# A decoder layer on one core: attention's x turned by a transfer instead of TensorE, and the keys scaled earlier

## What is computed

```python
x = x + mamba(layernorm(x))              # in-projection, causal conv, one 64-token chunk, gated norm, out-projection
x = x + xattn(layernorm(x), ctx_2048)    # 16 query heads, 4 key/value heads of 128
x = x + ffn(layernorm(x))                # 256 -> 1024 -> 256, activations rounded to 8 bits, ternary weights

def xattn(h, e):
    q = (h @ Wq + bq).reshape(..., 16, 128)
    k = (e @ Wk + bk).reshape(..., 4, 128)
    v = (e @ Wv + bv).reshape(..., 4, 128)
    q, k = rmsnorm(q) * qn_w, rmsnorm(k) * kn_w
    p = softmax(q @ k.T / sqrt(128) + mask)
    return (p @ v) @ Wo
```

## Time and profile before

| | us |
|---|---|
| median of 3 runs | 1190.26 (1189.74 to 1191.51) |
| the profiled execution | 1191.23 |
| its span | 1189.5 |
| TensorE busy | 1119.2 (94%) |
| VectorE busy | 1005.5 (85%) |
| GpSimd busy | 935.8 (79%) |
| ScalarE busy | 819.7 (69%) |

### The profile page before, as it was taken

How to read it: one execution, slowest core, us unless ns; L and a number is a source line. 1 busy time by engine, 2 the same in 40 slices (tenths; PEclk the granted TensorE clock), 3 DMA queues, 4 the chain that set the end, 5 groups by cost and what they waited for, 6 DMA issues and landing times.

```text
span 1189.5 us, 34826 instructions
## 1 busy us (share of the span) xinstructions
PE 1119.2 (94%) x11405; PEld 983.7 (83%) x11405; DVE 1005.5 (85%) x2509; ACT 819.7 (69%) x2066; POOL 935.8 (79%) x1514
## 2 busy tenths in 40 slices
PE   4889999999999999999999999999999999999964
PEld 3678888898888889888888988888898888888753
DVE  4766898898889889888988988898898889888666
ACT  4586777677667767766776776677677667766641
POOL 4788788888888888888888888888888888878651
PEclk8899999999999999999999999999999999999987
DMA  8311101111110111111011111101111110121000
GB/s 297 87 50 24 33 17 31 37 37 35 33 37 15 29 37 37 35 33 37 15 29 37 37 35 33 37 15 29 37 37 35 33 37 15 29 35 30 22 9 23
DMA packets 103306, 46.31 MB, mean 39 GB/s; under 512 B 80352, under 2 KB 101600, under 8 KB 103008
## 3 DMA queue, kind: packets, MB, share of 16 engines
q1 hardware_dynamic: 100336, 45.75, 14.8%
q10 hardware_dynamic: 2928, 0.03, 0.1%
HBM read 23.93 MB, written 4.19 MB: 24 GB/s over the span
## 4 chain that ended last, share of the span: by engine, by line
PE 66%; DVE 13%; ACT 13%; issue 4%; POOL 2%; DMA 1%; ACTq 1%; POOLq 0%; DVEq 0%; SPq 0%
PE bank L1800 18%; PE bank L1882 5%; PE bank L1860 5%; PE bank L1718 4%; PE bank L1690 4%; PE bank L1691 4%; PE bank L1692 4%; DVE hh L1389 3%; DVE hh L1382 3%; ACT kb L875 3%; PE bank L1813 3%; PE bank L1940 2%; PE bank L1707 2%; PE bank L1870 2%; PE bank L1762 2%
## 5 line engine op out<-in xcount | busy, mean ns | idle before, releaser
L1800 PE MATMUL bank<-xcT,wq 128*128 128x128 f32 x2048 | 234.1, 275 | 2.2 <-ACT xcT L862 2.2
L1800 PEld LDWEIGHTS bank<-xcT,wq 128*128 128x128 f32 x2048 | 231.2, 192 | 2.9 <-issue 2.5
L1223 DVE SCALAR_TENSOR_TENSOR xc<-bank,cw,xc 128x124 f32<-128x124 f32 (+2 forms) x576 | 163.7, 339 | 11.6 <-ACT xc L831 3.0
L1690 PE MATMUL bank<-wo_hi,o_hi 128*128 128x256 f32 x512 | 149.5, 292 | 1.1 <-DVE o_lo L1312 1.1
L1691 PE MATMUL bank<-wo_lo,o_hi 128*128 128x256 f32 x512 | 143.7, 281 | 0.0
L1692 PE MATMUL bank<-wo_hi,o_lo 128*128 128x256 f32 x512 | 143.3, 280 | 0.0
L887 ACT ACTIVATE qT<-bank,bqT 128x128 f32<-128x128 f32 x384 | 109.6, 372 | 41.0 <-PE bank L1800 41.0
L530 POOL TENSOR_TENSOR pr<-pr,mask 128x512 f32<-128x512 f32 x64 | 79.9, 1270 | 38.1 <-DVE pr L1331 38.0
L1690 PEld LDWEIGHTS bank<-wo_hi,o_hi 128*128 128x128 f32 x512 | 96.4, 188 | 1.5 <-DVE o_lo L1312 1.4
L1691 PEld LDWEIGHTS bank<-wo_lo,o_hi 128*128 128x128 f32 x512 | 96.7, 189 | 0.1
L1692 PEld LDWEIGHTS bank<-wo_hi,o_lo 128*128 128x128 f32 x512 | 96.5, 188 | 0.0
(11 more groups left out here) (239 smaller groups left out, 3414.5 us busy)
## 6 DMA issues: line engine op xcount, KB each, us to landing
x_in<-in_x SPq DMA_DIRECT2D x32, 128.0 KB, 2.1
c_in<-in_ctx SPq DMA_DIRECT2D x32, 128.0 KB, 2.1
x_m<-in_x SPq DMA_DIRECT2D x32, 128.0 KB, 2.2
out<-x SPq DMA_DIRECT2D x32, 128.0 KB, 1.7
wq<-in_L_xattn_Wq SPq DMA_DIRECT2D x1, 2048.0 KB, 14.1
stage<-in_L_xattn_Wo SPq DMA_DIRECT2D x2, 1024.0 KB, 8.4
w_in<-in_L_attn_W_in SPq DMA_DIRECT2D x1, 1024.0 KB, 6.3
qT<-in_L_ffn_w_gate SPq DMA_DIRECT2D x1, 1024.0 KB, 12.9
```

The costliest lines, as they stand in the source:

```text
L1223: last = v.scalar_tensor_tensor(out=o, in0=src, scalar=cw[:, j, TAPS - 1 - back:TAPS - back], in1=o, op0=ALU.mult, op1=ALU.add)
L1690: mm(out, left[0], right[0], start=first, stop=False)
L1800: last = mm(x_Qbank[g][:, (n % 4) * P:(n % 4 + 1) * P], wq[:, c, n * HD:(n + 1) * HD], xcT[:, c, :], start=(c == 0), stop=(c == DC - 1))
```

## The change

Attention's x takes the transfer way from tile 4 on. ScalarE's `x_split_halves` writes planes into a free part of q2's buffer, SP's `turn_x` turns them, and ScalarE's `x_join_halves` writes xcT. `x_transpose` and `x_T_copy` remain for tiles 0 to 3 only. SP's order becomes turn f, turn x, turn c, turn m, turn h. On ScalarE, `x_khat` moves ahead of everything that follows the copy of x_f, and `m_tanh_z` ahead of `m_tap_bc`; then come the splits of x, c and m, the tanh, kT's copy, the join of x, the two copies of residuals (`x_keep`, `x_hold`) and the join of c. On VectorE `x_norm` moves from the end of the iteration to just before the conv of bc; on GpSimd its reciprocal root moves ahead of the feed-forward part's. Queries of group 2, which use bank X2, now wait for kT's copy, since the transpose that did so is gone. VectorE's other work, the scaling of the feed-forward part and the residuals among it, keeps its place.

```diff
+        x_halves = c_flat[:, 2 * D:3 * D].bitcast(U16)
+        x_halvesT = c_flat[:, 3 * D:4 * D].bitcast(U16).rearrange("p (g n) -> p g n", g=2 * DC)
-        M_TURN, C_TURN = 4, 2
+        M_TURN, C_TURN, X_TURN = 4, 2, 4
...
+            def turn_x(t):
+                count(sp, s["x_planes"], t - X_TURN + 1)
+                sp.sem_inc(s["sp_waited"].sem, 1)
+                count(sp, s["x_turned"], (t - X_TURN) * 16)
+                sp.sem_inc(s["sp_waited"].sem, 1)
+                sp.dma_start_transpose(x_halvesT, x_halves).then_inc(s["x_turned"].sem, 16)
...
                     turn_f(i - 3)
+                if not isinstance(i, int) or X_TURN <= i < TILES:
+                    turn_x(i)
+                if not isinstance(i, int) or C_TURN <= i < TILES:
+                    turn_c(i)
                 if not isinstance(i, int) or M_TURN <= i + 2 < TILES:
                     turn_m(i + 2)
-                if not isinstance(i, int) or C_TURN <= i < TILES:
-                    turn_c(i)
                 if not isinstance(i, int) or 2 < i < TILES + 2:
                     turn_h(i - 3)
...
                     x_khat(xa)
+                if m is not None:
+                    x_norm(m)
                 if f is not None:
                     f_rms(f)
-                if m is not None:
-                    x_norm(m)
...
+            def x_split_halves(t):
+                after(act, s["x_xn"], t + 1)
+                count(act, s["x_turned"], (t - X_TURN) * 16)
+                sc.copy(x_halves.rearrange("p (g n) -> p g n", g=2),
+                        x_xn[:].bitcast(U16).rearrange("p (n g) -> p g n", g=2)).then_inc(s["x_planes"].sem, 1)
+
+            def x_join_halves(t):
+                count(act, s["x_turned"], (t - X_TURN + 1) * 16)
+                after(act, x_Q[3], t)
+                after(act, s["x_TT"], t)
+                sc.copy(xcT[:, 0:DC, :].rearrange("p c n -> p (c n)").bitcast(U16).rearrange("p (n g) -> p g n", g=2),
+                        x_halvesT.rearrange("p (g c) n -> p g (c n)", g=2)).then_inc(s["x_TT"].sem, 1)
...
-                if xa is not None:
+                if xa is not None and isinstance(xa, int) and xa < X_TURN:
                     x_T_copy(xa)
...
+                if xa is not None:
+                    x_khat(xa)
                 if mn is not None:
+                    m_tanh_z(mn)
                     m_tap_bc(mn)
+                if m is not None and (not isinstance(m, int) or m >= X_TURN):
+                    x_split_halves(m)
                 if m is not None:
                     c_split_halves(m)
                 if ms is not None:
                     m_split_halves(ms)
                 if mn is not None:
-                    m_tanh_z(mn)
-                if xa is not None:
-                    x_khat(xa)
-                if mn is not None:
                     m_tanh_bc(mn)
                 if xa is not None:
                     x_kT_copy(xa)
+                if m is not None and (not isinstance(m, int) or m >= X_TURN):
+                    x_join_halves(m)
+                if xa is not None:
+                    x_keep(xa)
+                if m is not None:
+                    x_hold(m)
                 if m is not None:
                     c_join_halves(m)
-                if xa is not None:
-                    x_keep(xa)
-                if m is not None:
-                    x_hold(m)
...
             def x_norm(t):
-                after(dve, s["x_T"], t)
+                if isinstance(t, int) and t <= X_TURN:
+                    after(dve, s["x_T"], t)
+                else:
+                    count(dve, s["x_planes"], t - X_TURN)
                 normalise(t, x1[:], x_mv, x_xn, s["x_rstd"], s["x_xn"])
...
                     m_silu_z(mn)
+                if m is not None:
+                    x_norm(m)
+                if mn is not None:
                     m_conv_bc(mn)
...
                     m_silu_bc(mn)
-                if m is not None:
-                    x_norm(m)
...
+                elif g == 2:
+                    after(pe, s["x_kT"], t)
...
-                if xa is not None:
+                if xa is not None and isinstance(xa, int) and xa < X_TURN:
                     x_transpose(xa)
```

More of the change, by code:

```diff
@@ L220, in decoder_layer @@
           m_tap m_convb+m_conva m_tb+m_ta m_bc+m_xs m_G m_Gm+m_Ma m_Xtr m_Xdt m_xd
-          m_Y m_y+m_yf m_sq m_ssy m_v4+m_ry m_out m_x1 m_planes m_turned c_planes c_turned c_xT f_qturned
+          m_Y m_y+m_yf m_sq m_ssy m_v4+m_ry m_out m_x1 m_planes m_turned c_planes c_turned c_xT f_qturned x_planes x_turned
           x_hold x_copy x_stats+x_mean x_veps+x_rstd x_xn x_T x_TT x_K+x_V x_kb+x_vb x_ksq x_kv+x_rk+x_kh
@@ L1147, in body @@
                     x_kT_copy(xa)
-                if m is not None:
-                    c_join_halves(m)
+                if m is not None and (not isinstance(m, int) or m >= X_TURN):
+                    x_join_halves(m)
                 if xa is not None:
@@ L1153, in body @@
                     x_hold(m)
+                if m is not None:
+                    c_join_halves(m)
             act.wait_ge(s["c_round"].sem, 1)
```

## The result

The changed kernel takes 1199.48 us (1199.25 to 1199.96) where the kernel before, run beside it, takes 1190.88 us: 1.0073 of its time, 95% interval 1.0056 to 1.0091. That is 8.6 us slower, on the side that was forecast and inside the range, and further than the 2.7 us of the forecast. The profiled span is 1198.0 us.

A forecast was written before the change was run, and what follows sets the result against it. TensorE, busy 94%, was taken as the bound, with SP's queue deciding after the change: 0.81 us gained an iteration is given back, and 26 iterations x 0.1 add 2.6 us, giving a forecast median of 1193.0 us, range 1179 to 1201.

The forecast's parts named there:

- Keys and x off TensorE: TensorE: keys' turn starts 0.59 us sooner and two turns of x go, 0.22 us; together 0.81 us an iteration.
- SP's queue is what I expect to decide: SP's issues: h goes 0.9 us later than VectorE alone would allow, so the whole 0.81 us gain is given back.
- some 20: TensorE at the down product: a new regular wait for h_q, 0.7 to 1 us each, some 20 us in all.
- The chain over h: Residual through x_xn, split, SP's turns and landing to the down product: 12.58 us; period 0.09 us longer.
- the one beside it: Late x_in load through VectorE's statistics to xdt: xdt late by 0.4 us at most, against 0.2 us of slack.
- My sign for this: TensorE at L1762 waiting for xdt by over 0.3 us an iteration would show the forecast wrong on the slower side.
- The two chains together: Chain over h and late x_in: 0.1 us an iteration, with 0 and 0.3 as the ends.
- the third case: Late x_in decides through xdt: 0.4 us an iteration, distinctly slower, 1201 us; chance 0.19.
- the first case: TensorE's wait moves from kb to h_q, period unchanged or a little longer: 1188 to 1198 us; chance 0.52.
- the weak joint: ScalarE's kT copy ends at 627.42, TensorE wants it at 627.61; just fits, up to 0.1 us if it slips.
- The rule on turning transfers: If SP were held no longer than by a load, part of the gain stays: second case, 1177 us, chance 0.27.

The follow-up runs named there:

- early keys alone: Kernel before with only ScalarE's scaling of the keys, then the tanh of z, moved ahead of the tap of bc: 1175.5 us.
- The swap of the order: Changed kernel with SP's order x, c, h, m instead of x, c, m, h: 1209.5 us.
- the early load: Changed kernel with the x_in load issued behind the turn of f (for tile i+3) instead of behind the turn of h: 1194.6 us.
- the pair: Changed kernel with both SP's order x, c, h, m and the x_in load behind the turn of f: 1180.8 us.
- the doubled turn: Changed kernel with x's planes turned a second time, into an unused part of the buffer, right behind the first turn: 1270.6 us.
- all thirteen kernels: The kernel before, the changed kernel and all the follow-up kernels, whose times run from 1169.7 to 1270.6 us.
- the fastest kernel: Changed kernel with SP's order x, c, h, m, the early x_in load, and VectorE's gating of z behind that of bc; residual unmoved: 1169.7 us.

## Why the prediction was right, and where its size was off

**Keys and x off TensorE.** 0.59 us was 0.58 (early keys alone), 0.22 was 0.23. Right.

**Where the gain goes.** "SP's queue is what I expect to decide" holds: L1881 without idle time, L1973 waiting for the transfer of h, SP no longer waiting for VectorE with h, VectorE waiting ahead of its statistics. The swap of the order, the early load, the pair and the doubled turn all hang on it. But the wait at L1973 is 0.54 us where 0.7 to 1 was said: TensorE comes to it later, since the scores take 2.45 us instead of 2.08. The 22.7 us in all fit "some 20" only with the waits outside the loop.

**The chain over h** was 12.58 us and is 12.70. Its terms, forecast and measured: residual to x_xn 4.67 and 4.57 (623.08 to 627.65); split 0.66 and 0.73; planes to issue and the three turns 4.48 and 4.55; issue to product 2.77 and 2.85. The turns aren't evenly spaced: 1.51, 1.38 and 1.50 where I took 1.39, 1.39 and 1.48. The down product is 0.21 us later behind the residual (12.70 against 12.49) where 0.09 was forecast. Errors of up to 0.1 us at each term, and the result is what is left between two long sums. With the load repaired, where this chain decides by itself, the period is 0.14 us above the one before.

**The step that failed is the one beside it.** "xdt is late by 0.4 at most, against 0.2 us of slack": there were no 0.2 us. The distance from xdt's end to the product is 0.26 us before (609.56 to 609.82), 0.25 in the changed kernel (612.68 to 612.93), and 0.25 in the run with h before m, where the wait is marked (620.31 to 620.56). On the mean of the iterations between 300 and 950 us it is 0.25 to 0.27 us in all thirteen kernels. It is the handover itself. VectorE's only reserve was its 0.16 us of waiting for decay ahead of mw, and in the changed kernel mw starts without a wait, at 611.20. I had counted that one as well, so I took off 0.36 where 0.16 was there. xdt ends 0.33 us later behind the first residual than before, as forecast ("0.4 at most"), and all of it reaches TensorE. My sign for this, a wait of over 0.3 us at L1762, did not show (0.15 us is marked), because TensorE was late itself. The two chains together cost 0.35 us a period and not 0.1. My upper end for them was 0.3; the range of the time held because it was stretched for the third case, which is luck as far as the first case goes: its own range, 1188 to 1198, didn't hold.

**The third case**, decided by the late x_in, is the one whose mechanism sets the period, and it had a chance of 0.19. Its load comes as late as forecast (11.82 us behind the residual; 11.78 forecast), and its 0.4 us an iteration is nearer to the 0.35 than the forecast's 0.1. The idle times that it supposed not to be free were free, though; what was missing was the slack at xdt. And it is not the whole: the chain over h is only 0.21 us shorter, and with the load repaired the kernel is still slower than before. I had treated the two as rivals, but they run side by side.

**Not in the prediction at all:** the residual that holds up the second half of the scores. In the changed kernel it only shortens the wait at L1973, but it costs 0.32 us a period once SP is repaired. It would have been found by asking, for VectorE's 0.33 us shift, who waits for each instruction behind it, and not only for h.

**kT**, named as the weak joint, held: its copy ends at 629.79 + 0.67 = 630.46 in ScalarE's list, and the scores start at 630.69 without a wait for it.

```profile
629.79 0.67 ACT L905 ACTIVATE kT<-bank,qk_w 128x512 f32<-128x512 f32 x1
```

**The rule on turning transfers.** The Trainium skill, "Advanced Engine Details and Errata", section "X-Bar Transpose (TRN2)", says that transposing DMAs are as fast as regular ones. For the landing the changed kernel's trace nearly agrees, 2.4 us for a turn and 2.1 for a load; for the issue it doesn't, 1.19 against 0.35 us. Here the issue decided.

## What to carry to other kernels

A queue that issues transfers is an engine with a list like any other. Price a transfer by how long its issue holds the queue, and go through everything queued behind it, the plain loads too; here a 1.2 us issue, harmless to its own consumer, undid 0.8 us a period through two others.

When two chains are about equally long, repair both before judging: single edits to the changed kernel showed -5 and +10 us, the pair -19. And a constant distance between a producer's end and a consumer's start, the same in kernels that wait and in kernels that don't, is a handover and no slack.

An order written by hand can fail on either side: moving the residual forward by one instruction was worth nothing, with 0.6 us less work ahead of it it cost some 3 us, and leaving it while the work ahead of it moved away gave the fastest kernel, 1169.7 us.

## What the runs showed of the hardware

- A wait of 0.54 us at the down product in every loop iteration left TensorE's granted clock at full speed. One of 1.97 us in the same place was followed by the 1.2 GHz level in 16 of 24 iterations, in one of them with a granted clock of 0.52 over the next three microseconds. An SP issue that added 1.4 us to the wait so cost 2.5 us a period on the mean.
- Turning transfers of one queue, issued 1.38 to 1.51 us apart, four in a row, land as fast as f's, which stands alone (2.4 us, h 2.7 us as before), and a plain load behind four of them lands in the same 2.1 us as behind three. The queue's length was felt at issue only. The list of DMA issues of the changed kernel, columns as in the earlier trace rows:

```profile
x_in<-in_x SPq DMA_DIRECT2D x32, 128.0 KB, 2.1
...
q<-q SPq DMA_TRANSPOSE x58, 2.4
...
h_q<-h_q SPq DMA_TRANSPOSE x31, 2.7
f_qT<-f_qb SPq DMA_TRANSPOSE x29, 2.4
```

- From the end of VectorE's xdt to TensorE's product of it, 0.25 to 0.27 us pass on the mean in all thirteen kernels, whether a wait is marked there or not.
